# Both convolutions packed into their weights, and run in halves of an image pair

## The reference

```python
x = x + L0(gn(x));  x = x + L1(gn(x))
# L0: 4 parallel branches of two 3x3 convolutions, both with binarised input and weights
out = bconv3x3(tile(x, 4), w1, groups=4)          # sign(x) with sign(w1): 64 -> 256 channels
out = relu(batchnorm(out, bn1))                   # only its sign is used: > 0 or not
out = bconv3x3(out, w2, groups=4)                 # 256 -> 256, in 4 groups of 64
out = (batchnorm(out, bn2) * lambdas).sum over the 4 branches;  L0 = relu(out + gn(x))
# L1: mid = x * mask;  atten = sigmoid(conv7x7([mean_c(mid), max_c(mid), mask]))
#     L1 = relu(5 * (instance_norm(mid * atten) * gamma + beta))
```

## Time and profile before

| | |
|---|---|
| time, median of 3 runs | 300.83 us (300.37 to 301.81) |
| profiled execution, its own time | 298.91 us |
| its span, first to last instruction | 297.1 us |
| PE, DVE, ACT, POOL busy | 238.0, 216.5, 159.2, 182.9 us |
| granted TensorE clock, mean | 0.918 |

### The profile page before, as it was taken

The page is one execution under the profiler, slowest core; times in us unless marked ns, Lnnn a source line. Parts: engine busy times, 40 slices in busy tenths (PEclk is TensorE's granted clock), DMA queues, the critical chain, the costliest instruction groups (busy, mean ns, idle before and its releaser), DMA issues.

```text
span 297.1 us, 6991 instructions
## 1 busy us (share of the span) xinstructions
PE 238.0 (80%) x2742; PEld 152.4 (51%) x2742; DVE 216.5 (73%) x523; ACT 159.2 (54%) x191; POOL 182.9 (62%) x215
## 2 busy tenths in 40 slices
PE   8293998698998989897988798979879896866850
PEld 4262754355565556554654565456536454643640
DVE  3349642759776797989888887998696869656362
ACT  2432251275757657575758575756665774444121
POOL 2300410224534577798787969896979697967762
PEclk9668777689999999999999999999999999988775
DMA  7990000713015321632173115122512331141014
GB/s 199 307 310 14 0 2 2 182 48 110 3 57 160 114 55 58 183 97 103 58 209 113 61 61 160 57 56 85 135 54 56 119 103 57 57 160 57 0 56 162
DMA packets 11947, 28.86 MB, mean 97 GB/s; under 512 B 2286, under 2 KB 3566, under 8 KB 11758
## 3 DMA queue, kind: packets, MB, share of 16 engines
q1 hardware_dynamic: 11481, 28.13, 30.5%
q10 hardware_dynamic: 432, 0.29, 0.4%
HBM read 21.79 MB, written 6.61 MB: 96 GB/s over the span
## 4 chain that ended last, share of the span: by engine, by line
PE 56%; DVE 23%; issue 11%; DMA 3%; ACT 3%; POOL 3%; SPq 1%; POOLq 0%; DVEq 0%; ACTq 0%
PE big L901 16%; PE big L887 13%; PE big L918 10%; DVE gate L619 5%; PE small L947 5%; PE small L936 4%; DVE RD L634 4%; DVE bnst L563 4%; DMA X<-in_x 3%; DVE S L625 2%; PE small L991 2%; ACT word L471 2%; DVE red L658 2%; PE small L863 1%; POOL o L359 1%
## 5 line engine op out<-in xcount | busy, mean ns | idle before, releaser
L901 PE MATMUL big<-S,w2t 64*64 64x392 f16 x1152 | 57.3, 353 | 7.4 <-DVE S L625 7.4
L936 PE MATMUL small<-cs,o 128*112 128x130 f32 x224 | 35.1, 303 | 26.6 <-POOL o L359 19.3
L887 PE MATMUL big<-E,w1t 64*128 64x392 f16 x576 | 55.2, 334 | 0.0
L634 DVE TENSOR_SCALAR RD<-word 128x784 f16<-128x784 uint16 x32 | 33.1, 1035 | 22.2 <-ACT word L471 22.2
L901 PEld LDWEIGHTS big<-S,w2t 64*64 64x64 f16 x1152 | 33.9, 113 | 26.2 <-DVE S L625 5.1
L936 PEld LDWEIGHTS small<-cs,o 128*112 128x112 f32 x224 | 28.8, 190 | 35.7 <-POOL o L359 25.2
L359 POOL TENSOR_TENSOR o<-o,mask_b 128x784 f32<-128x784 f32 x16 | 35.6, 2226 | 15.4 <-ACT o L491 15.4
L471 ACT ACTIVATE word<-big 128x784 int32<-128x784 f32 x32 | 26.1, 815 | 27.1 <-PE big L901 27.1
L377 POOL TENSOR_TENSOR X<-X,acc 128x784 f32<-128x784 f32 x15 | 29.3, 1957 | 13.9 <-ACT acc L485 13.9
L918 PE MATMUL big<-RD,wa 128*64 128x392 f16 x384 | 36.1, 339 | 0.6 <-DVE RD L634 0.6
L887 PEld LDWEIGHTS big<-E,w1t 64*128 64x128 f16 x576 | 25.7, 95 | 21.0 <-issue 4.5
(11 more groups left out here) (118 smaller groups left out, 336.1 us busy)
## 6 DMA issues: line engine op xcount, KB each, us to landing
X<-in_x SPq DMA_DIRECT2D x16, 392.0 KB, 6.0
mask_b<-mask_rows SPq DMA_DIRECT2D x32, 196.0 KB, 3.5
out<-o SPq DMA_DIRECT2D x16, 392.0 KB, 2.4
att_b<-attention_rows SPq DMA_DIRECT2D x28, 196.0 KB, 3.7
o<-in_w SPq DMA_DIRECT2D x3, 576.0 KB, 9.1
o<-in_masks SPq DMA_DIRECT2D x1, 512.0 KB, 10.6
cs<-in_cst SPq DMA_DIRECT2D x1, 385.0 KB, 11.9
o<-in_sel SPq DMA_DIRECT2D x1, 343.0 KB
```

The costliest lines, as they stand in the source:

```text
L634: dve.tensor_scalar(RD[:, t % 2, hh, 1, :], low2[:, hh, :], LIFT, 1.0 / UNIT, ALU.subtract, ALU.mult).then_inc(split, 1)
L887: mm = pe.matmul(acc[:, LOW + HALF * hh:LOW + HALF * (hh + 1)], w1t[64 * hh:64 * hh + 64, s, q * P:(q + 1) * P], window(RH * hh, s // 3, s ...
L901: mm = pe.matmul(acc[64 * q:64 * q + 64, LOW + HALF * r:LOW + HALF * (r + 1)], w2t[64 * r:64 * r + 64, s, 64 * q:64 * q + 64], window(RH * ...
L936: mm = pe.matmul(small[1 - n % 2][0:CP, at:at + P + 2], o[:, t, CP * j:CP * (j + 1)], cs[:, K_ID:K_ID + P + 2], start=True, stop=True)
```

## The change

- First convolution: the two branches of a channel pair are packed in the weights instead (`w1t` = 2046 * sign of one + sign of the other, made once by `join_weights`); `sign_x` writes straight into `E`; `join` and `pack_signs` go. `conv1(t, hh)` does both images for a part of the rows: 15 rows of each for hh = 0 and 13 for hh = 1 (420 and 364 columns), 18 matmuls each, with 64 input and 128 output rows as before.
- Gates: the high half of the word goes through a steep Sigmoid on ACT (`high_gates`), the low half through one DVE `tensor_scalar` (`low_gates`); they write separate gates `S`.
- Second convolution: two output channels are packed in the weights (`w2t` = 1024 * a + b). `conv2(t, hh)` is now 9 taps x 2 x 2 x 2 = 72 matmuls with 64 input and 32 output rows, 144 in a step where there were 72. It writes one PSUM buffer, `c2`, so each waits for the other's `words2`.
- `mix(t, hh)` is 24 matmuls with 64 input and 32 output rows, where it was 12 with 128 and 64. `y` has its own PSUM buffer.
- The order: the loop runs k = 1 to 22 and takes in all that trailed; turn, attention, `relu_block` and `add_x` stand one step later, `stats_o`, `last_relu` and `scale3` too. The zero matmuls behind the loop go, those ahead of it are fewer. `make_u` stands last on POOL but for `mask_column`.
- Ahead of the loop: the bands come by DMA instead of `sel` and 56 matmuls; `w1` is read once (576 KB where it was 1152 KB) through ACT's queue; the scales of `mix` are one DVE instruction; picks are repeated on POOL.

```diff
@@ gpsimd, vector, scalar: what each makes of the words
+            def high_gates(t, hh):                                   # ACT
+                    act.wait_ge(worded1, 2 * t + hh + 1)
+                    wait(act, conv2_done, 2 * t - 2)
+                    act.activation(gate_rows(t, hh, 0), by_rows(high_of(word1_of(hh))), ACT.Sigmoid,
+                                   bias=thr_high[:, :], scale=STEEP).then_inc(gated_high, 1)
-                dve.tensor_scalar(gate0[:, q, :], high1[:, q, :], thr[:, q:q + 1], GATE, ALU.is_gt, ALU.mult)\
-                dve.scalar_tensor_tensor(inside(S2[:, t % 2, q, :]),
-                                         low1[:, q, :].rearrange("p (h w) -> p h w", w=W), thr_low[:, q:q + 1],
-                                         gate0[:, q, :].rearrange("p (h w) -> p h w", w=W), ALU.is_gt, ALU.add)\
+                    dve.tensor_scalar(gate_rows(t, hh, 1), by_rows(low_of(word1_of(hh))), thr_low[:, :], None,
+                                      ALU.is_gt).then_inc(gated_low, 1)
@@ tensor: the second convolution
+                pe.wait_ge(gated_low, 2 * t + hh + 1)
+                pe.wait_ge(gated_high, 2 * t + hh + 1)
+                wait(pe, worded2, 2 * t + hh)
+                for s in range(KS):
                     for r in range(2):
+                        for i in range(2):
+                            for q in range(2):
+                                at = Q32 * (2 * i + q)
+                                mm = pe.matmul(c2[at:at + Q32, LOW + HALF * r:LOW + HALF * (r + 1)],
+                                               w2t[64 * r:64 * r + 64, s, q, :],
+                                               window(RH * half_of(i, hh), RH, s, S[64 * r:64 * r + 64, t % 2, i, q, :]),
...
@@ gpsimd, the loop
+            for k in range(1, STEPS):
+                if k in TERMS_AT:
+                    power1(batch(k + 1))
+                add_x(k - 2)
+                if (k - 5) % 2:
+                    attend(k - 5)
+                    scale3(k - 6)
+                    power2(k - 2)
+                else:
+                    scale3(k - 6)
+                    power2(k - 2)
+                    attend(k - 5)
+                last_sum(k - 6)
+                make_u(k - 2)
                 mask_column(k - 2)
@@ scalar, the loop
+            for k in range(1, STEPS):
+                relu_block(k - 2)
+                words1(k, 0)
+                high_gates(k, 0)
                 words2(k - 1, 1)
+                high_sums(k - 1, 1)
                 sign_x(k + 1)
+                last_relu(k - 6)
+                words1(k, 1)
+                high_gates(k, 1)
                 normalise2(k - 2)
                 words2(k, 0)
+                high_sums(k, 0)
+                sigmoid(k - 3)
@@ vector, the loop
+                attend_last(k - 5)
+                stats_o(k - 6)
                 if k < 3:
                     stats_x(2 * k + 2)
                     stats_x(2 * k + 3)
                 else:
                     stats_x(k + 5)
+                low_gates(k, 0)
...
+                stats_x1(k - 2)
+                low_sums(k - 1, 1)
+                terms2(k - 2)
+                reduce_chunks(k - 3, 0)
+                reduce_chunks(k - 3, 1)
+                low_gates(k, 1)
+                reduce_chunks(k - 3, 2)
+                low_sums(k, 0)
+                finish_block(k - 1)
+                last_sum(k - 6)
@@ tensor, the loop
+            for k in range(1, STEPS):
                 conv1(k, 0)
+                conv2(k - 1, 1)
+                if k == 1:
+                    turn_mask()
+                mix(k - 1, 0)
+                group_2(k - 2)
+                if k == 3:
                     pe.wait_ge(mask_rows, 2)
+                turn(k - 3, 0)
+                turn(k - 3, 1)
                 conv1(k, 1)
+                turn(k - 3, 2)
+                conv2(k, 0)
+                attention(k - 3)
                 mix(k - 1, 1)
...
+                spread_attention(k - 4)
```

More of the change, by code:

```diff
@@ new lines, in half_of, with first_sums, second_sums, word1_of @@
+        def half_of(i, step):
+            return step if i == 0 else 1 - step
+        def first_sums(step):
+            n = ROWS[step] * W
+            return c1[:, 512 - n:512 + n]
+        def second_sums():
+            return c2[:, LOW:LOW + HW]
+        def word1_of(step):
+            return word1[:, step, 0:2 * ROWS[step] * W]
+        def block_sums():
+            return y[:, LOW:LOW + HW]
+        def low_of(sums):
+            return sums.bitcast(U16).rearrange("p (n two) -> p n two", two=2)[:, :, 0]
@@ L368, in attend @@
             def attend(t):
-                if has(t):
+                if has(t) and t < POOL_ATTENDS:
                     pool.wait_ge(u_ready, t + 1)
@@ L401, in _ @@
             pool.wait_ge(half_ready, 1)
[L402 removed]
             pool.wait_ge(prep, 1)
             pool.tensor_tensor(rs[:, :], pv[:, :], mhalf[:, :], ALU.pow).then_inc(prep_pow, 1)
+            power1(0)
             clear_borders()
             power1(1)
[L407 to L408 removed]
             pool.wait_ge(cleared, CLEARED)
+            repeat_picks()
             pool.wait_ge(mask_mix, 8)
[L411 to L415, removed]
[L416 to L437 removed]
+            for k in range(1, STEPS):
[12 more added lines that the diff above has]
+                make_u(k - 2)
+                mask_column(k - 2)
         @block.scalar
@@ L445, in sign_x @@
                 act.wait_ge(mean1, batch(t) + 1)
[L446 to L451, removed]
                 if t == 0:
                     act.wait_ge(cleared, 1)
-                act.wait_ge(joined, t + 1)
-                wait(act, conv1_done, t * 2 - 2)
-                act.activation(inside(E[:, t % 2, :]), sums("join").rearrange("p (h w) -> p h w", w=W), ACT.Copy)\
-                   .then_inc(packed, 1)
@@ L521, in _ @@
+            act.wait_ge(w1_joined, 3)
+            act.activation(w1t[:, 6:9, :].rearrange("p k o -> p (k o)"), y[:, 0:3 * P], ACT.Copy).then_inc(w1_ready, 1)
             act.wait_ge(w2_in, 16)
             act.activation(w2s[:, :, :].rearrange("p s o -> p (s o)"), w2f, ACT.Sign).then_inc(w2_signs, 1)
+            words1(0, 0)
+            high_gates(0, 0)
             sign_x(1)
-            for q in range(2):
-                words1(0, q)
-            pack_signs(1)
+            words1(0, 1)
+            high_gates(0, 1)
@@ L535, in _ @@
                 normalise2(k - 2)
-                words1(k, 1)
-                relu_block(k - 1)
-                pack_signs(k + 1)
-                last_relu(k - 5)
                 words2(k, 0)
-                high_half(k, 0)
-                sigmoid(k - 2)
-            words2(15, 1)
-            high_half(15, 1)
-            normalise2(14)
-            relu_block(15)
-            last_relu(11)
-            act.wait_ge(cst_rest, 16)
-            repeat_picks()
-            normalise2(15)
-            last_relu(12)
@@ L954, in keep_clock @@
                 for _ in range(n):
-                    pe.matmul(big[2][:, LOW:512], warm[:, 0:P], warm[:, :], start=True, stop=True)
+                    pe.matmul(small[0][:, 0:HALF], warm[:, 0:P], warm[:, :], start=True, stop=True)
             def spread_attention(t):
+                if not has(t) or t < POOL_ATTENDS:
+                    return
                 if t == POOL_ATTENDS:
@@ L1064, in _ @@
-                for n in range(3):
-                    turn(k - 2, n)
-                conv2(k, 0)
-                conv2(k, 1)
-                attention(k - 2)
-                if k == 1:
-                    pe.wait_ge(band_ready, 2)
+                turn(k - 3, 2)
+                conv2(k, 0)
+                attention(k - 3)
+                mix(k - 1, 1)
                 if k in (2, 6, 10):
                     group_1(batch(k + 2))
-            group_2(14)
-            mix(15, 0)
-            mix(15, 1)
```

621 lines of the change are left out of this document (285 added, 336 removed).

## The result

The changed kernel took 314.36 us (median of 4 runs, 312.81 to 317.66), the kernel before 300.60 in the same session (300.13 to 301.81). The ratio is 1.043, 95% interval 1.038 to 1.049: slower, within the range forecast and 2.9 us above the predicted 311.5. The profiled execution took 314.67 us for a span of 312.9.

The account below looks back on a forecast made before the run. Bound taken: program order and waits across engines from finish_block to finish_block. Stretches of 48.5, 12.7, 191.1, 11.8 and 43.7 give a span of 307.8 us; with 1.8 around it 309.6, as median 311.5; range 296 to 324.

Parts of the forecast that it names:

- The loop: Path from finish_block to finish_block: 14.2 us in odd steps, 15.5 in even ones from k = 6; chance 0.60.
- the 13 steps: Steps 3 to 15: eight of 14.2 us and five of 15.5, 191.1 us in all.
- rival 1: Loop does not meet make_u and last_sum: 13 steps take 176.4 us, total 296.8 (290 to 299); chance 0.20.
- the idle time ahead of group_2: PE in the loop: idle about 2 us before group_2, a sign that the forecast is right.
- F(0): Start of finish_block of step 0: between 44.8 and 52.9 us, taken as 48.5; before the change 49.82.
- the first conv1: Ahead of the loop: conv1(0, 0) can start some 5 us sooner, near 14 us.
- Step 2: From finish(0) to finish(1), without a turn: 12.7 us, finish(1) at 61.2 against 66.76 before.
- Step 16: From finish(14) to finish(15), no convolution but conv2(15, 1): 11.8 us, finish(15) at 264.1.
- From F(15) on: From finish_block of step 15 to the end: 22.9 us to the first attend_last, then 20.8; 43.7 in all.
- Rival 2: conv2 runs four tiles at a time, 3.1 us a half: 324 us, from 318 to 335; chance 0.10.
- rival 3: PE's sequencer at 62 ns per matmul makes PE's step 17.6 us, the time about 350; chance 0.02.

Follow-up runs that it names:

- e3: Changed kernel with 14 (even k) or 8 (odd k) zero matmuls in PE's gap ahead of group_2, order unchanged: 306.25 us, ratio 1.022.
- e2: Changed kernel with conv1(k, 1) moved ahead of group_2 on PE: 290.15 us, ratio 0.966.
- e5: Changed kernel with POOL's make_u multiplying only 98 of its 784 columns by the mask: 298.71 us, ratio 0.986.
- e8: Changed kernel with conv1(k, 1) ahead of group_2, reduce 2 ahead of low_gates(k, 1), last_sum behind the next pair's statistics: 281.86 us, ratio 0.938.
- e9: Changed kernel with low_gates(k, 0) behind stats_x1(k - 2) on DVE instead of ahead of it: 305.64 us (10 runs), ratio 1.009.
- e1: Changed kernel with ACT's normalise2(k - 2) moved behind words2(k, 0) and high_sums(k, 0): 319.86 us, ratio 1.056.
- e10: Kernel of e8 with finish_block(k - 1) ahead of low_sums(k, 0) on DVE: 282.59 us, ratio 0.945.

## Why the prediction was right, and where it was off

**The loop.** Right. "All of it is program order or a wait, from finish_block of one step to finish_block of the next" is what the trace shows, link by link: in step 12, counted from F = 199.14, add_x ends at F+3.9 (3.96 walked), group_2 starts at F+5.62 (5.63), last_relu ran from F+8.3 to 9.4 (8.6 to 9.65), attention started at F+12.5 (12.4). low_sums took 1.6 us or more in ten of the thirteen steps; in the other three, 9, 13 and 15, it took 1.0 to 1.3, and they ended at 13.3 to 13.7 for 14.2. e3, which only holds the clock up, took 189.9 us for the 13 steps against 191.1 walked. e2 shows the other side: with conv1(k, 1) off this path they take 176.7. That 176.7 is close to rival 1's 176.4 is chance: e2 gets there by another order, with the meetings still in it.

**Where it was off: the walk priced PE at full clock throughout.** The step is "Statistics to group_2 1.32; group_2 0.32; two turns 1.6 ... conv1(k, 1) 1.5". The prediction had the idle time ahead of group_2 (about 2 us forecast; 1.3 to 2.0 in odd steps from 5 on, 2.5 to 3.3 in even ones and in step 3), but took it for idle time only. The clock fell behind it in step 3 and in every even step, the turns then took up to 2.92 and conv1 2.9, and the 13 steps 9.3 us more than walked: 5.0 of it in steps 3 and 4 (16.4 and 16.9 for 14.2), 4.7 in the even steps from 6 on, and -0.3 in the odd ones from 5 on. e3 shows it: with the clock full steps 3 and 4 took 14.9 and 14.0. In step 12 this cost little, because a meeting fell out in exchange: low_gates(k, 1) came late enough to miss last_sum, took 0.60, and the step ended at 15.6 after all. The -0.3 hides a second term that the walk lacks: in steps 3, 7 and 11 POOL does `power1` ahead of add_x, and DVE `make_bias1` ahead of the statistics, and group_2 starts at F+6.6 instead of F+5.6; so steps 7 and 11 took 15.0 and 15.3. Also missing are the waits of attend for the DMA that brings its attention rows, six of them and 6.7 us together, as here in step 11:

```profile
193.01 1.86 POOL L396 TENSOR_TENSOR o<-o,att_b 128x784 f32<-128x784 f32 x1 [0.72 <-DMA att_b<-attention_rows]
```

What they cost the end no run shows.

**Head and tail.** F(0) came 3.0 us earlier than the forecast's middle, near its lower bound; the first conv1 began at 11.97, not 14. Step 2 was 12.87 for 12.7. Step 16 was 12.6 for 11.8. From F(15) on it was 41.6 for 43.7, the last sums of the three rounds 6.1 and 5.3 apart for 6.35 and 5.4. Head and tail, -5.2 together, hid part of the +9.3 by luck, and the span came to 312.9 for 307.8. That the medians are nearer, 314.36 for 311.5, is luck too: the forecast went from the profiled execution, at 298.91, to the median of 300.83, and the kernel after has hardly such a difference (314.67 and 314.36).

**The costs of single parts.** conv2 at 1.72 a half, high_gates at 0.91 and 1.00 for 0.9, the 1.59 of conv1's second half for 1.5: right. Rival 2 (four tiles at a time) and rival 3 (62 ns per matmul) are out: 72 matmuls in 1.72 us are 24 ns each. The 62 ns is what "TensorE: Matmul & The Clock Gate" in the Trainium skill (section "Wait — 56ns, not 53.3ns?") has for the hardware decoder off; no run here shows it. The eight 64x32 tiles of "TensorEngine Tiling (Array Packing)" in the Trainium skill (Available Configurations) agree with the 1.72 us. Rival 1 (a loop that misses the meetings, 296.8) did not come by itself. e5, which cuts make_u short, is at 298.7, but its loop took 188.1 where rival 1 has 176.4; its even steps stayed at 15.1 to 15.7, for some 14.0, and head and tail make up the rest.

**What was not tried.** Whether the changed kernel's even steps would keep their clock with less on POOL ahead of the statistics; nor what the packing alone brings over the old layout in e8's order: the kernel before was not put into it. And the split of e5's 16 us between the meeting and POOL's shorter list stays open, and e2, e5 and e9 each move a wait and the clock at once; only e3 moves the clock alone.

## What to carry to other kernels

When a change halves a unit of work, write out the loop from one step's end to the next in issue order, and look for what now stands between two halves: here group_2 and two turns ahead of conv1(k, 1), and moving one call took out 24 us, more than all the change cost. Idle time of the matrix engine is to be priced twice, as idle and as what follows it at half clock. A wait taken away by moving its cause later (e1), or by moving the waiting instruction (e10), can come back at the start of the next step; follow the moved instruction until its engine is idle again.

## What the hardware showed

- Filling PE's wait with zero matmuls made the kernel faster by 8.1 us (314.36 to 306.25): the granted clock went from 0.91 in the loop (110 to 254 us) to 1.00 (110 to 250). In the changed kernel's loop the lower clock had followed waits of PE of 2.54 us (step 14) to 3.28 us (step 12), and stayed for 3.4 or 6.8 us.
- A waiting 16-bit DVE instruction is not always next: low_gates took 3.02 us in e10 across two POOL instructions that stood back to back, while in the changed kernel, at 201.93, it got in between add_x and attend (1.59 us).
- 72 matmuls of 64x32 tiles over 392 columns took 1.72 us at full clock, 24 ns for each.
